# Local sums of five blocks made per tile in the second stage, from x1 reloaded out of HBM

## The reference

```python
x = x + pooled_attention(x)          # masked softmax inside blocks and across them
x = x + du_dt(x)                     # the step that the change touches
x = x + layernorm(x + relu(x @ Wd + bd) @ Wu + bu) * g + b      # adapter by profile id
x = x + recurrent(x)                 # gates, two exponential moving averages, output norm

def du_dt(y):                        # zX, zY, zR: one number for each batch
    lap_x = y[:, :, left] - 2 * y + y[:, :, right]     # along channels, reflected at the ends
    lap_y = y[:, above, :] - 2 * y + y[:, below, :]    # along positions, reflected at the ends
    return zX * lap_x + zY * lap_y + zR * y * (1 - y)
```

## Time and profile before

| | |
|---|---|
| median of 3 runs | 737.13 us |
| span of the profiled execution | 734.0 us |
| TensorE busy | 672.6 us (92%), 2808 matmuls |
| VectorE busy | 541.1 us (74%) |
| ScalarE busy | 353.3 us (48%) |
| GpSimd busy | 177.6 us (24%) |
| share of the chain that ended last | TensorE 80%, DMA 6%, VectorE 5%, GpSimd 3%, ScalarE 3% |
| moved by DMA | 87.87 MB |

### The profile page before, as it was taken

How to read it: one execution, slowest core, us unless ns; L and a number is a source line. 1 busy time by engine, 2 the same in 40 slices (tenths; PEclk the granted TensorE clock), 3 DMA queues, 4 the chain that set the end, 5 groups by cost and what they waited for, 6 DMA issues and landing times.

```text
span 734.0 us, 7942 instructions
## 1 busy us (share of the span) xinstructions
PE 672.6 (92%) x2808; PEld 493.9 (67%) x2808; DVE 541.1 (74%) x737; ACT 353.3 (48%) x710; POOL 177.6 (24%) x220
## 2 busy tenths in 40 slices
PE   4969979265899999999999999999999999999996
PEld 1545444134677877778687868786877787787884
DVE  2665888766898688759766976697668758875965
ACT  1143376445356625653474357344724563465235
POOL 5002456656152300420132022102310220031001
PEclk9989999767899999999999999999999999999999
DMA  7896799679930970295039305820880040004001
GB/s 212 292 367 185 162 236 306 197 136 339 327 66 0 167 121 0 67 188 90 1 95 191 58 1 127 169 49 22 150 160 14 0 115 2 0 10 106 0 2 57
DMA packets 52470, 87.87 MB, mean 120 GB/s; under 512 B 8256, under 2 KB 10304, under 8 KB 52430
## 3 DMA queue, kind: packets, MB, share of 16 engines
q0 software_dynamic: 16896, 33.56, 27.7%
q1 hardware_dynamic: 32046, 53.79, 20.8%
q10 hardware_dynamic: 3488, 0.01, 0.3%
HBM read 64.27 MB, written 23.09 MB: 119 GB/s over the span
## 4 chain that ended last, share of the span: by engine, by line
PE 80%; DMA 6%; DVE 5%; POOL 3%; ACT 3%; issue 1%; SPq 1%; POOLq 0%; ACTq 0%; DVEq 0%
PE bank L1055 21%; PE bank L1057 20%; PE bank L1056 20%; PE bank L1095 3%; PE bank L1111 3%; PE bank L956 3%; PE bank L1158 2%; PE bank L1120 2%; DMA xr<-beside_scratch 2%; DMA beside_scratch<-xb 2%; PE bank L1085 2%; PE bank L1051 2%; DMA local_scratch<-xts 2%; DMA xts<-in_xT 1%; POOL xts L546 1%
## 5 line engine op out<-in xcount | busy, mean ns | idle before, releaser
L1556 DVE TENSOR_TENSOR_SCAN tr<-alpha,carry,tr 128x512 f32<-128x512 f32 x48 | 58.9, 1268 | 0.0
L593 POOL TENSOR_TENSOR rs_a<-ss_a,consts 128x1 f32<-128x1 f32 x32 | 10.5, 329 | 197.8 <-ACT hb L744 196.9
L1550 DVE SCALAR_TENSOR_TENSOR tr<-wgb,blend_w,mod 128x512 f32<-128x512 f32 x64 | 46.0, 750 | 10.7 <-ACT mod L769 9.9
L1055 PE MATMUL bank<-xh,wg_l 128*128 128x512 f32 x128 | 52.9, 413 | 0.0
L1055 PE MATMUL bank<-th,wg_l 128*128 128x512 f32 x128 | 52.0, 406 | 0.0
L1056 PE MATMUL bank<-xl,wg_h 128*128 128x512 f32 x128 | 50.4, 394 | 0.0
L1057 PE MATMUL bank<-xh,wg_h 128*128 128x512 f32 x128 | 50.3, 393 | 0.0
L1057 PE MATMUL bank<-th,wg_h 128*128 128x512 f32 x128 | 50.1, 391 | 0.0
L1056 PE MATMUL bank<-tl,wg_h 128*128 128x512 f32 x128 | 49.9, 390 | 0.0
L546 POOL TENSOR_TENSOR xts<-xb 128x2040 f32<-128x2040 f32 x8 | 29.3, 3662 | 65.0 <-DVE xb L1445 52.8
L1051 PE MATMUL bank<-xb,probT 128*128 128x512 f32 x64 | 39.3, 700 | 4.4 <-DVE xb L1445 4.4
(11 more groups left out here) (247 smaller groups left out, 1984.9 us busy)
## 6 DMA issues: line engine op xcount, KB each, us to landing
x2b<-beside_scratch POOLq DMA_DIRECT2D x12, 1024.0 KB, 9.1
xr<-rows_scratch POOLq DMA_DIRECT2D x10, 1024.0 KB, 10.3
xb<-in_x SPq DMA_DIRECT2D x8, 1024.0 KB, 14.4
beside_scratch<-xb SPq DMA_DIRECT2D x8, 1024.0 KB, 9.5
result<-xr SPq DMA_DIRECT2D x7, 1024.0 KB, 4.4
local_scratch<-xts SPq DMA_DIRECT2D x6, 1024.0 KB, 11.2
x2b<-local_scratch SPq DMA_DIRECT2D x6, 1024.0 KB, 5.6
x2b<-rows_scratch POOLq DMA_DIRECT2D x6, 1024.0 KB, 15.1
```

The source lines that it names most:

```text
L1055: pe.matmul(acc, wl, xh_, start=start, stop=False)
L1550: ve.scalar_tensor_tensor(t[:, d], w, blend_w[:, d, k:k + 1], mod[:, d], ALU.mult, ALU.mult).then_inc(tr_in, 1)
L1556: ve.tensor_tensor_scan(t[:, d], alpha[:, 1 + d:2 + d].broadcast_to([P, GN]), t[:, d], 0.0 if first else carry[:, k, 1 + d:2 + d], ALU.mul ...
```

## The change

The local parts of blocks 0 to 2 are made as before, except that block 2's is written directly into the buffer of x2 (`x2b0`). For blocks 3 to 7 the first stage makes no local part. It stores x1 itself into a scratch (`x1_scratch`, `store_x1`), and ScalarE writes the scaled block into a buffer of its own instead of over x1. In the second stage, each of the 20 tiles of these blocks is loaded into one tile buffer `late_y` (`load_late`), mixed by ScalarE into the x2 buffer (`late_mix`), summed left and right by GpSimd (`late_channels`), and multiplied and completed by VectorE (`late_by_local`, `late_stencil`). In group g three tiles of block g+3 are made, and the fourth at the start of group g+1. The bias row of that block is added after its fourth tile. `coef` and `wn2_rep` live for the whole program now, and `wn2_rep` is made with the small parameters at the beginning.

```diff
@@ SP
-                    store_beside(2)
-                    store_local(2)
+                    store_beside(2)
                     sp.dma_start(wg_st[:, KE:], chunks(wg)[:, KE:]).then_inc(w_in[1], 16)
-                    store_beside(3)
-                    load_x2(2)
-                    store_local(3)
...
+                    for n in (3, 4, 5):
+                        store_x1(n)
+                        store_beside(n)
+                    sp.wait_ge(x1_out[4], 16)
+                    sp.wait_ge(x1_out[5], 16)
                     sp.dma_start(ws_st[:], chunks(wsoma)).then_inc(w2_in[0], 16)
...
+                    def load_late(q, c):
+                        n = late_tile(q, c)
+                        if n == 0:
+                            sp.wait_ge(x1_done, B * NT)
+                        else:
+                            sp.wait_ge(late_v, n)
+                            sp.wait_ge(late_chan, 3 * n)
+                        sp.wait_ge(x1_out[q], 16)
+                        sp.dma_start(late_y[:], x1_rows(q)[:, c]).then_inc(late_in, 16)
...
                     for g in range(GROUPS - 1):
                         if g + 3 < GROUPS:
-                            load_x2(g + 3)
+                            for c in range(GT):
+                                load_late(g + 3, c)
                         sp.wait_ge(o_done, GT * g + GT)
@@ GpSimd
+                    def late_channels(q, c):
+                        po.wait_ge(late_in, 16 * (late_tile(q, c) + 1))
+                        if late_tile(q, c):
+                            po.wait_ge(late_done, late_tile(q, c))
+                        po.tensor_tensor(late_side[:, 1:E - 1], late_y[:, 0:E - 2], late_y[:, 2:E], ALU.add)\
+                          .then_inc(late_chan, 1)
...
                     for g in range(GROUPS):
+                        late = g + 3 < GROUPS
+                        if 0 < g and g + 2 < GROUPS:
+                            late_channels(g + 2, GT - 1)
+                            add_up_bias(g + 2)
                         if g + 2 < GROUPS:
                             add_before(g + 2)
@@ ScalarE
                     def scale_beside(n):
                         b = n // NG
-                        act.wait_ge(mix_v, n + 1)
-                        act.wait_ge(chan, 3 * (n + 1))
-                        act.activation(x1_of(n), x1_of(n), ACT.Identity, scale=coef[:, ZY, b:b + 1])\
+                        if n < HEAD_BLOCKS:
+                            act.wait_ge(mix_v, n + 1)
+                            act.wait_ge(chan, 3 * (n + 1))
+                        else:
+                            act.wait_ge(x1_done, GT * (n + 1))
+                        if n >= HEAD_BLOCKS + 2:
+                            beside_landed(act, (n - 2) // NG, (n - 2) % NG)
+                        act.activation(scaled_of(n), x1_of(n), ACT.Identity, scale=coef[:, ZY, b:b + 1])\
                            .then_inc(beside_done, 1)
+
+                    def late_mix(q, c):
+                        n, b = late_tile(q, c), q // NG
+                        act.wait_ge(late_in, 16 * (n + 1))
+                        if q == HEAD_BLOCKS:
+                            act.wait_ge(local_done, HEAD_BLOCKS)
+                        else:
+                            act.wait_ge(x3_done, GT * (q - 1))
+                        act.activation(x2_of(q)[:, c], late_y[:], ACT.Identity, bias=coef[:, MID, b:b + 1],
+                                       scale=coef[:, NEG_ZR, b:b + 1]).then_inc(late_u, 1)
@@ VectorE
+                        for d in range(2):
+                            ve.tensor_copy(wn2_rep[:, d], wn2_col[:, d:d + 1].broadcast_to([P, P])).then_inc(wn2_set, 1)
...
+                    def late_by_local(q, c):
+                        n = late_tile(q, c)
+                        ve.wait_ge(late_u, n + 1)
+                        ve.tensor_tensor(x2_of(q)[:, c], x2_of(q)[:, c], late_y[:], ALU.mult).then_inc(late_v, 1)
+
+                    def late_stencil(q, c):
+                        n, b = late_tile(q, c), q // NG
+                        ve.wait_ge(late_v, n + 1)
+                        ve.wait_ge(late_chan, 3 * (n + 1))
+                        ve.scalar_tensor_tensor(x2_of(q)[:, c], late_side[:], coef[:, ZX, b:b + 1], x2_of(q)[:, c],
+                                                ALU.mult, ALU.add).then_inc(late_done, 1)
```

More of the change, by code:

```diff
@@ L217, in build_program @@
         rows2_set = sem("rows2_set")
+        x1_out = [sem(f"x1_out{q}") for q in range(GROUPS)]
+        late_in = sem("late_in")
+        late_u = sem("late_u")
+        late_v = sem("late_v")
+        late_chan = sem("late_chan")
+        late_done = sem("late_done")
         N1, PRE, CTX, MOD = 1, (5, 0, 2, 5), (6, 1, 3, 6), (7, 4)
@@ L630, in _ @@
                             add_shift(g + 1)
[L631 to L632 removed]
+                        if late:
+                            late_channels(g + 3, 1)
                         for c in range(GT):
+                            if late and c == 2:
+                                late_channels(g + 3, 2)
                             rstd(o_ss, ss_o, EPSILON_4, rs_o, GT * g + c, o_p, o_rs, c)
@@ L898, in _ @@
                         adapted = g < LAST
+                        late = g + 3 < GROUPS
                         n1_gelu(g)
+                        if 0 < g and g + 2 < GROUPS:
+                            late_mix(g + 2, GT - 1)
                         keep_ctx(g, 0)
@@ L1637, in _ @@
                     x1(1, 1)
-                    by_local(3)
-                    stencil(3)
                     x1(1, 2)
@@ L1651, in _ @@
                         ln_apply(0, c)
-                    by_local(4)
-                    stencil(4)
                     x1(1, 8)
@@ L1658, in _ @@
                     x3_lo(0)
-                    by_local(5)
                     x1(1, 12)
                     x1(1, 13)
-                    stencil(5)
                     x1(1, 14)
                     x1(1, 15)
-                    by_local(6)
-                    stencil(6)
-                    by_local(7)
-                    stencil(7)
-                    for d in range(2):
-                        ve.tensor_copy(wn2_rep[:, d], wn2_col[:, d:d + 1].broadcast_to([P, P])).then_inc(wn2_set, 1)
                     assert n["p"] == S_PARAMS, n["p"]
@@ L1673, in _ @@
                         adapted = g < LAST
+                        late = g + 3 < GROUPS
+                        last_tile = 0 < g and g + 2 < GROUPS
+                        if last_tile:
+                            late_by_local(g + 2, GT - 1)
                         logits(g, 0)
+                        if last_tile:
+                            late_stencil(g + 2, GT - 1)
                         traces(g, 0)
@@ L1706, in _ @@
                             product_lo(g, k - 1)
+                            if late and k == 1:
+                                late_by_local(g + 3, 0)
+                                late_stencil(g + 3, 0)
                         product_lo(g, KE - 1)
                         if adapted:
-                            x3_lo(g + 1)
+                            x3_lo(g + 1, (0, 1))
+                            if late:
+                                late_by_local(g + 3, 1)
+                                late_stencil(g + 3, 1)
+                            x3_lo(g + 1, (2, 3))
                         for c in range(GT):
+                            if late and c == 3:
+                                late_by_local(g + 3, 2)
+                                late_stencil(g + 3, 2)
                             out_apply(g, c)
```

108 lines of the change are left out of this document (50 added, 58 removed).

## The result

The changed kernel took 728.12 us, the median of 6 runs (727.25 to 729.94), beside 736.75 us for the kernel before on the same chip: ratio 0.9891, 95% interval 0.9865 to 0.9916. It is faster by 1.1%, where 3% was forecast, and the time lies 1.1 us above the predicted range.

The account below looks back on a forecast made before the run. TensorE was taken as the bound, so only its pauses counted. From the 734.0 us span, 20.4 (earlier gating matmul) and 1.5 (clock) came off, 0 was added for new work: 712.1, plus 3.1 gave 715.2 us; range 706 to 727.

Parts of the forecast that it names:

- Normalising block 0: First stage, block 0: last ln_apply, held by weight_low(2), ends near 139, about as late as before (137.9); bounds 133 and 139.6.
- Evicting its transposes: Block 0's first eviction on ScalarE, freed of operations ahead, starts at 140.1 instead of 145.85; gain 5.75 us.
- The rest of x1: VectorE's last x1 of block 0 ends at 153.7; group 0 starts then instead of 164.01, 10.3 us earlier.
- wn2 replicated early: Before group 0's gating matmul: the wn2 pause goes; TensorE's 11.3 us of matmuls from 153.7 end at 165.0.
- What is late next: Group 0's gelu behind weight_hi(0): ws load taken as 11 us, gelu ends at 164.3, just hidden behind 165.0.
- 1.5 us for the cold clock: Group 0 after its gating matmul: without the 10.2 us pause, half the slow-matmul loss credited, 1.5 us; bounds 0 and 3.0.
- The added work: Late tiles in groups 0 to 4: no TensorE stall, 0 us; bounds 0 and 2.1 per boundary, 10.5 in all.
- The sum: Whole kernel: forecast span 712.1 us plus 3.1 us around the span gives 715.2 us.
- The second rival: Group boundaries: one late load each in traffic, 7.5 us, stalls 2.1 us at five boundaries; 725.7 us, chance 0.21.
- The fourth rival: Before group 0's gating matmul: ws load takes 15 us or more, 3.6 us lost, 718.8; inside likeliest case (0.55).

Follow-up runs that it names:

- the guard: Changed kernel plus one GpSimd wait: weight_low(2) after block 0's four ln_apply, 720.42 us; where product_lo is discussed, second late tile's channels after four product_lo, 719.13 us.
- four to six edits: Changed kernel with gelu before weight_hi(0), soma awaiting ws_l alone, two GpSimd waits: 710.23 us; plus block 0's rstd earlier: 709.76; plus block 7's scaling earlier: 707.47.

## Why the prediction was wrong

*Normalising block 0* was right as a mechanism and in size: ln_apply(0,3) was held by weight_low(2) until 137.94 (139 forecast), and the guard shows its price, 4.15 us. *Evicting its transposes* (139.20 against 140.1) and *The rest of x1* (152.43 against 153.7) were right within 1.3 us. *wn2 replicated early*: the first 36 matmuls took 8.6 us, not 11.3, at a granted clock of 1.00 instead of 0.73, so TensorE was ready at 161.06, 3.9 us before my 165.0. It gained nothing by that, since the gelu ended only at 170.48. And the early copies, which I counted on, were not needed for the gain.

*What is late next* is the first step that failed. The chain was named rightly, ScalarE's weight_hi(0) in front of the gelu; the load was mis-sized: 11 us taken, with bounds of 6.7 and 15.3 from the earlier trace rows, 18.2 measured, outside both. I had named the two accumulating transfers and still took the middle of two durations measured in other company; they were worth 9.8 us, as moving them behind the load shows. So 15.03 us came instead of 20.4. The *1.5 us for the cold clock* failed with it: it supposed no pause, and a pause of 9.47 us stayed (granted clock 0.50 from 170.5 to 176).

*The added work*, priced at 0, is the second failure. I looked for the tight place at the fourth tile's load. That path is quiet: the 20 loads took 2.7 us in the median, and TensorE waited for none. The price came from GpSimd's channels of the second tile, 1.54 us, which I had sized (about 1.4 us) and given no price. Their cost falls on VectorE, at the one product_lo that TensorE awaits with little slack. I had used exactly this lock for ln_apply, with the earlier trace rows, and not asked where else GpSimd would now run beside VectorE. Measured 4.64 us in groups 1 to 3. Group 0 lost 1.87 us: 0.9 are TensorE's waits for product_lo, and the rest is busy time of TensorE (73.4 us instead of 72.4), at a mean granted clock of 0.96 instead of 0.97, which the guard does not explain.

The account, in spans: 5.4 us at the load, 1.5 at the clock, 6.5 in groups 0 to 3 less 0.2 elsewhere, 13.2 in all; forecast 21.9, came 8.7. (The sum's 3.1 us around the span was about 1 us too much: runs with a span on record have 1.7 to 2.1.) The second rival named nearly the measured time, 725.7, with late loads as its cause; that cause is refuted, so the agreement is chance. The fourth rival, a load of 15 us or more, happened and was larger than its 3.6 us. With four to six edits on the places found, the time fell to 707 to 710 us: a gain of the forecast size can be had, but with edits that the change did not contain.

What stays open: why the changed kernel took 3 us less when it was measured again, what the rest of group 0's 1.87 us is, and whether fewer bytes between 140 and 176 us would free group 0's 78 us.

## What to carry to other kernels

When work moves to an idle engine, list what its operations lock, not only what they take: put GpSimd's two-input operations beside VectorE instructions that have slack, and hold them back with a semaphore where they haven't. When a pause has two causes of nearly the same length, removing one pays the difference only; look at what each engine waits for next in its own queue, above all at a weight copy that stands in front of an unrelated activation. Price a transfer by what has been issued ahead of it in the new order, accumulating transfers above all, not by its row in the old one.

## What was unexpected of the hardware

From 120 to 170.5 us the accumulating queue moved 3.16 MB for 37.7% of the 16 engines, the plain one 10.31 MB for 55.0%: 11.9% against 5.3% per MB, so an accumulated megabyte occupied the engines 2.2 times as long. And a store's issue on SP, mostly 0.36 us, took 7.1 to 8.7 us in the changed kernels between 142 and 162 us, which delays everything behind it in SP's order. Full engines are not enough for that: before the change, stores were issued in 0.36 us at 160.92 and 162.46, between 160 and 170 us with a DMA share of 1.09. In the long cases the two accumulating transfers were in flight and SP had issued 2 MB or more in the 12 us before; with these transfers moved away a store at 147.07 took 0.36 us. Which of this counts is not shown.
